# Two-term matmuls for five of fc2's sixteen groups, with the scales applied to the sum in PSUM, and every y_hi copy on ScalarE

## The reference

```
attn_in = tanh(x @ W1 + b1)                       # 512 -> 128
scores  = attn_in @ v
p       = softmax(where(mask, scores, -1e30))     # prefix, postfix or cloze mask by sequence
pooled  = (p @ x) / count(mask)
h       = layernorm(pooled) * gamma + beta
y       = silu(h @ dequant(fc1_q, fc1_scales) + fc1_bias)      # 512 -> 2048
z       = y @ dequant(fc2_q, fc2_scales) + fc2_bias            # 2048 -> 512
out     = x + pooled + 0.5 * z
# dequant: (q - 128) * scale, one scale for each group of 128 rows of the weight and each column
```

## Time and profile before

| | |
|---|---|
| median of 3 runs | 1396.38 us (1396.19 to 1396.42) |
| the profiled execution | 1397.07 us, its span 1395.4 us |
| PE busy | 1362.2 us (98% of the span), 6243 matmuls |
| DVE busy | 967.0 us (69%) |
| ACT busy | 895.6 us (64%) |
| POOL busy | 198.7 us (14%) |
| granted TensorE clock | 0.994 of full on average |

### The profile page before, as it was taken

One profiled execution on the slowest core, in us unless ns is written; L12 is line 12 of the kernel. 1 busy time (PEld: TensorE's weight loads), 2 busy tenths in 40 slices (PEclk: granted clock), 3 DMA queues, 4 the chain that ended last, 5 costly groups with the idle time before them and its releaser, 6 DMA issues.

```text
span 1395.4 us, 20229 instructions
## 1 busy us (share of the span) xinstructions
PE 1362.2 (98%) x6243; PEld 1075.6 (77%) x6243; DVE 967.0 (69%) x1923; ACT 895.6 (64%) x1415; POOL 198.7 (14%) x156
## 2 busy tenths in 40 slices
...
DMA packets 271437, 82.15 MB, mean 59 GB/s; under 512 B 247530, under 2 KB 248196, under 8 KB 270852
## 3 DMA queue, kind: packets, MB, share of 16 engines
...
...
## 4 chain that ended last, share of the span: by engine, by line
PE 66%; SPq 16%; DVE 10%; issue 5%; DMA 3%; ACT 1%; ACTq 0%; DVEq 0%
PE y_ps L1110 12%; PE z_ps L1137 11%; PE y_ps L1111 11%; PE z_ps L1139 11%; PE z_ps L1138 11%; SPq L394 10%; SPq L349 6%; DMA h_cols<-scratch 2%; DVE h_rows L862 2%; DVE hT_lo L874 1%; PE a_ps L1020 1%; PE a_ps L1069 1%; PE a_ps L1071 1%; PE a_ps L1070 1%; PE a_ps L1021 1%
## 5 line engine op out<-in xcount | busy, mean ns | idle before, releaser
L600 ACT ACTIVATE y_ps<-y_ps,ratio 128x512 f32<-128x512 f32 x768 | 474.7, 656 | 342.0 <-PE y_ps L1111 340.3
L1110 PE MATMUL y_ps<-hT_hi,w 128*128 128x512 f32 x1016 | 403.1, 397 | 15.6 <-DVE hT_lo L874 8.9
L1137 PE MATMUL z_ps<-w_hi,y_hi 128*128 128x512 f32 x1024 | 409.4, 400 | 0.0
L1139 PE MATMUL z_ps<-w_hi,y_lo 128*128 128x512 f32 x1024 | 400.2, 391 | 0.0
L1138 PE MATMUL z_ps<-w_lo,y_hi 128*128 128x512 f32 x1024 | 400.1, 391 | 0.0
L1111 PE MATMUL y_ps<-hT_lo,w 128*128 128x512 f32 x1016 | 396.9, 391 | 0.0
L904 DVE CAST y_hi<-y_f 128x512 fp32r<-128x512 f32 x248 | 120.5, 486 | 263.9 <-ACT y_f L594 161.9
L1110 PEld LDWEIGHTS y_ps<-hT_hi,w 128*128 128x128 f32 x1016 | 191.3, 188 | 76.7 <-issue 13.9
L594 ACT ACTIVATE y_f<-y_ps,vec_cols,mant 128x512 f32<-128x512 f32 x256 | 185.2, 775 | 94.3 <-PE y_ps L1111 92.3
L1137 PEld LDWEIGHTS z_ps<-w_hi,y_hi 128*128 128x128 f32 x1024 | 192.9, 188 | 58.7 <-issue 19.4
L1138 PEld LDWEIGHTS z_ps<-w_lo,y_hi 128*128 128x128 f32 x1024 | 192.8, 188 | 42.7 <-issue 3.6
...
## 6 DMA issues: line engine op xcount, KB each, us to landing
...
```

The costliest lines, as they stand in the source:

```text
L600: nc.scalar.activation(y_ps[k % 2][:], y_ps[k % 2][:], ACT.Copy, scale=ratio[:, c * NF + k:c * NF + k + 1]).then_inc(scaled, 1)
L1110: mm(o, w, hT_hi[:, c, :], start=(c == 0), stop=False, skip_group_check=True)
L1137: mm(z_ps[r][:], y_hi[k % 2][:, rows], w2_hi[:, k, :], start=(k == 0), stop=False)
L1139: last = mm(z_ps[r][:], y_lo[k % 2][:, rows], w2_hi[:, k, :], start=False, stop=(k == NF - 1))
```

## The change

Groups 1, 6, 7, 10 and 11 of fc2 (WHOLE) are done like fc1: their weight holds (q - 128) times a power of two, exact in fp32r, so the hi by lo matmul (L1138) is left out for them. After each of these groups VectorE multiplies the whole sum so far, in PSUM, by a ratio of mantissas (`rescale_z`, four multiplications of 128x512 a group). The weights of the groups between them are divided by the mantissa that is still to come, and the factor 0.5 moves into these units. VectorE, GpSimd and one DMA to device memory make the units in the prologue (`scale_masks`, units_dram), and the units and ratios are loaded from there. The first of two row blocks is multiplied one slot after its matmuls, the other in the slot behind that; fc2 of the next group waits for them (z_scaled).

All y_hi copies move to ScalarE: for one group behind the two SiLUs, for the other at the start of the second slot after. VectorE's `split_y` keeps the subtraction. GpSimd's bias waits for h_ready instead of hT_done, in sequence 0 for more of fc2. In sequence 0 the steps L2 and W2 of the five groups go.

```diff
+    WHOLE = (1, 6, 7, 10, 11)
+    EARLY = 3
+    SEGMENTS = ((0, 1, 1), (2, 6, 6), (8, 10, 10))
...
-        DVE_LATE = {0: [("L2", 1), ("D1", 4)], 1: [("D2", 2)], 3: [("L2", 2)], 4: [("D2", 4)], 5: [("D1", 6)], 6: [("L2", 4)],
+        DVE_LATE = {0: [("D1", 4)], 1: [("D2", 2)], 3: [("L2", 2)], 4: [("D2", 4)], 5: [("D1", 6)], 6: [("L2", 4)],
...
             load_w1(0)
+            sp.wait_ge(units2, 1)
+            sp.dma_start(units_dram.rearrange("k (p j) -> p k j", p=Q), u2_c).then_inc(units2_out, 16)
+            sp.wait_ge(units2_out, 16)
+            load_w2_units(0)
+            load_ratios(z_ratio[:], 0, EARLY)
...
                 if J == 0 and is_first(a):
-                    pool.wait_ge(fc2_done, 4)
+                    pool.wait_ge(fc2_done, 10)
                 elif J == 0:
-                    pool.wait_ge(hT_done, a * ND + ND)
+                    pool.wait_ge(h_ready, a * NJ + NJ)
...
+            pool.wait_ge(masks2, 1)
+            for k0, k1, k in SEGMENTS:
+                step(g.tensor_tensor(u2_c[:, k0:k1, :], s2_c[:, k0:k1, :], i2_c[:, k:k + 1, :].to_broadcast([Q, k1 - k0, NC]), ALU.mult))
...
-            def y_hi_part(k):
-                act.wait_ge(silu_done, k + 1)
-                if k >= 2:
-                    act.wait_ge(fc2_done, k - 1)
-                copy(y_hi[k % 2][:], y_f[k % 2][:]).then_inc(yhi_even, 1)
+            def y_hi_part(b, k):
+                act.wait_ge(silu_done, b * NF + k + 1)
+                if k >= 2 or not is_first(b):
+                    act.wait_ge(fc2_done, b * NF + (k - 1))
+                copy(y_hi[k % 2][:], y_f[k % 2][:]).then_inc(yhi_done, 1)
...
                     ahead, k, c = fc1_slot(i)
+                    if i % 4 == 0:
+                        y_hi_part(b, i // 2 + 1)
...
-                    if is_first(b) and c == ND - 1 and not ahead:
-                        y_hi_part(k)
+                        if c == ND - 1:
+                            y_hi_part(b + ahead, k)
...
+            def scale_masks():
+                dve.wait_ge(s2_in, 16)
+                bits, mants = s2_c.bitcast(I32), m2_c.bitcast(I32)
+                link(v.tensor_scalar(u2_c[:, 0:NF, :].bitcast(I32), bits, 23, 23, ALU.logical_shift_right, ALU.logical_shift_left))
+                link(v.tensor_scalar(mants, bits, 9, 9, ALU.logical_shift_left, ALU.logical_shift_right))
+                link(v.tensor_tensor(mants, mants, ones[0:Q, 0:1].bitcast(I32).rearrange("p (k j) -> p k j", j=1).to_broadcast([Q, NF, NC]), ALU.bitwise_or))
+                v.reciprocal(i2_c, m2_c).then_inc(masks2, 1)
...
             def split_y(b, k):
-                dve.wait_ge(silu_done, b * NF + (k + 1))
-                if k >= 2 or not is_first(b):
-                    dve.wait_ge(fc2_done, b * NF + (k - 1))
-                if is_first(b) and k % 2 == 0:
-                    dve.wait_ge(yhi_even, k // 2 + 1)
-                else:
-                    v.tensor_copy(y_hi[k % 2][:], y_f[k % 2][:]).then_inc(yhi_done, 1)
-                    dve.wait_ge(yhi_done, (k + 1) // 2 if is_first(b) else b * NF + (k + 1) - NH)
+                dve.wait_ge(yhi_done, b * NF + k + 1)
                 v.tensor_tensor(y_lo[k % 2][:], y_f[k % 2][:], f32(y_hi[k % 2][:]), ALU.subtract).then_inc(split_done, 1)
+
+            def rescale_z(b, k, r):
+                if r < NJ - 1:
+                    dve.wait_ge(z_part, z_part_count(b, k, r))
+                else:
+                    dve.wait_ge(fc2_done, b * NF + (k + 1))
+                if is_first(b) and r == 0:
+                    dve.wait_ge(ratio_in, 16 if WHOLE.index(k) < EARLY else 32)
+                v.tensor_tensor(z_ps[r][:], z_ps[r][:], z_ratios[WHOLE.index(k)], ALU.mult).then_inc(z_scaled, 1)
...
                 for i in range(SLOTS):
-                    if i % 4 == 0:
-                        split_y(b, i // 2 + 1)
                     if i % 4 == 3 and i < SLOTS - 1:
                         split_y(b, (i + 1) // 2)
+                    if (i - 1) // 2 in WHOLE:
+                        for r in (2 * ((i - 1) % 2), 2 * ((i - 1) % 2) + 1):
+                            rescale_z(b, (i - 1) // 2, r)
+                    if i % 4 == 0:
+                        split_y(b, i // 2 + 1)
...
                 if k == 0 and not is_first(b):
                     pe.wait_ge(final_done, (b - 1) * NJ + (r + 1))
+                if k - 1 in WHOLE:
+                    pe.wait_ge(z_scaled, z_count(b, k - 1, r))
                 rows = slice(r * P, (r + 1) * P)
-                mm(z_ps[r][:], y_hi[k % 2][:, rows], w2_hi[:, k, :], start=(k == 0), stop=False)
-                mm(z_ps[r][:], y_hi[k % 2][:, rows], w2_lo[:, k, :], start=False, stop=False)
-                last = mm(z_ps[r][:], y_lo[k % 2][:, rows], w2_hi[:, k, :], start=False, stop=(k == NF - 1))
+                mm(z_ps[r][:], y_hi[k % 2][:, rows], w2_hi[:, k, :], start=(k == 0), stop=False, skip_group_check=True)
+                if k not in WHOLE:
+                    mm(z_ps[r][:], y_hi[k % 2][:, rows], w2_lo[:, k, :], start=False, stop=False, skip_group_check=True)
+                last = mm(z_ps[r][:], y_lo[k % 2][:, rows], w2_hi[:, k, :], start=False, stop=(k == NF - 1 or k in WHOLE), skip_group_check=True)
```

More of the change, by code:

```diff
@@ L127, in small @@
             return columns4[:, k * NJ:(k + 1) * NJ]
+        z_ratio = sb("z_ratio", [P, EARLY, D])
+        z_ratios = [z_ratio[:, j, :] for j in range(EARLY)] + [e1[1][:, j, :] for j in range(len(WHOLE) - EARLY)]
+        units_dram = nc.dram_tensor("units_dram", [NF + len(WHOLE), D], F32, kind="Internal").ap()
+        NC = D // Q
+        s2_c, m2_c, i2_c = (h_rows[0:Q, 1 + n, 0:NF * NC].rearrange("p (k j) -> p k j", k=NF) for n in range(3))
+        u2_c = h_rows[0:Q, 0, 0:(NF + len(WHOLE)) * NC].rearrange("p (k j) -> p k j", j=NC)
         pen_c = small()
@@ L230, in build @@
         powers_out = sem("powers_out")
+        s2_in = sem("s2_in")
+        masks2 = sem("masks2")
+        units2 = sem("units2")
+        units2_out = sem("units2_out")
+        ratio_in = sem("ratio_in")
+        z_part = sem("z_part")
+        z_scaled = sem("z_scaled")
         fc1_done = sem("fc1_done")
@@ L386, in _ @@
                 load_w2(g)
+            for k0 in w1_unit:
+                if k0 // NG == 1:
+                    sp.wait_ge(w1_unit[k0], 1)
+            sp.wait_ge(ratio_in, 16)
+            load_ratios(e1[1][:, 0:len(WHOLE) - EARLY, :], EARLY, len(WHOLE))
             def move_h(a):
```

58 lines of the change are left out of this document (39 added, 19 removed).

## The result

The changed kernel takes 1426.93 us (median of 4 runs, 1424.87 to 1431.66) against 1396.29 for the kernel before: ratio 1.0226, 95% interval [1.0211, 1.0241]. It is 2.3% slower. The profiled execution took 1431.66, its span is 1429.9, 34.5 more than before. It is the slowest of the four: they took 1431.66, 1427.27, 1426.60 and 1424.87 at mean granted clocks of 0.975, 0.980, 0.983 and 0.984.

The account below looks back on a forecast made before the run. It took PE's matmuls and a fixed DMA chain from slot 16 to 27 as bounds side by side. 1395.4 - 1.4 (14 sequences) - 4.5 (last) + 5 (prologue, sequence 0) + 1.5 (waits) gave span 1396, forecast 1397.5 us, range 1374 to 1421.

Parts of the forecast that it names:

- Cost of a multiplication of z: On DVE, one multiplication of z in PSUM takes 0.60 us, like the final addition; bounds 0.55 and 1.66.
- Rival (d): A multiplication in PSUM costs 0.72 us instead of 0.60; 12 on the path, +1.4 a sequence, 1418; chance 0.14.
- Slots 2 to 8: Group 1's multiplications delay y_lo(4), for which slot 8 waits: 1.04 us longer a sequence instead of 0.91 shorter.
- Rival (a): DVE keeps up better, slot 8 not waiting for y_lo(4): 1370 to 1383, or 1360; chance 0.22.
- Slots 12 to 16: PE saves 8 matmuls, 1.81 us a sequence; full DVE delays the last split of x, stall 0.36.
- Slots 16 to 27: xs_used 0.6 us earlier, but h waits for normalisation; slot 27 starts 0.07 earlier, PE waits there about 2.9.
- the chain: Fixed stretch from the column DMAs after slot 16 through the h DMAs and transposes to slot 27; 24.3 us before.
- rival c: The pause before slot 27 lowers TensorE's clock: 1.3 us in each of 14 sequences, 18 in all, 1416; chance 0.15.
- Slots 27 to 2: The y_hi(15) copy adds 0.27 us at slot 29; moving GpSimd's bias takes 0.3 off; -0.03 a sequence.
- Prologue and sequence 0: Making the units and 14 multiplications on a full DVE cost +5 us together, believable from +2 to +9.
- last sequence: With no conditioning work beside it, the last sequence saves its whole 4.53 us of matmuls.
- The sum itself: Over the whole kernel: 1395.4 - 1.4 - 4.5 + 5 = 1394.5, plus 1.5 for forgotten waits; said 1397.5.

Follow-up runs that it names:

- e9: The changed kernel with group 1 back to three matmuls, so four groups with two (6, 7, 10, 11): 1435.12 us, ratio 1.0288.
- e5: The changed kernel with GpSimd's residual addition of block 2 made to wait for the last xs_lo: 1420.58 us, ratio 1.0173.
- e1: The changed kernel plus 8 idle matmuls on PE in slots 20 to 23 of sequences 1 to 14: 1419.03 us, ratio 1.0165.
- e4: The kernel before with every y_hi made by ScalarE, three matmuls for every group, bias not moved: 1406.22 us, ratio 1.0076.

## Why the prediction was wrong

It forecast 1397.5 with a range of 1374 to 1421; 1426.93 is above both. Two terms of its sum failed: the stall behind slots 12 to 16, which it put at 0.36 us and which is 1.29, and the clock behind slot 27, which it left out of the sum and which cost 17.8 us. By its own steps:

- **Cost of a multiplication of z**: right. 0.690 us each, 0.60 from start to start: two in 1.29 (DVE's rows above). Rival (d) is out.
- **Slots 2 to 8**: right. DVE began y_lo(2) at 681.58, 2.72 behind slot 2 (forecast 2.70), y_lo(4) at 694.56, 15.70 behind it (15.63). Slot 2 to 9 is 17.94 us against 16.83 before: +1.1, forecast +1.04. Rival (a) is out. e9 takes 0.6 of it away.
- **Slots 12 to 16**: the saving was right (1.81 forecast; slot 12 to 16 is 10.01 instead of 11.78, -1.77). **The stall of 0.36 behind it was wrong, it is 1.29** (18.0 / 14). I had the slow y_lo beside GpSimd in the earlier trace rows, and used it for the bias, but did not ask which other instruction the shift of DVE's queue would push under the residual additions. e5 takes 0.97 of it away; the 0.31 that are left (4.4 / 14) are what the 0.36 was worked out for.
- **Slots 16 to 27**: the structure was right, its start was not. Counted from slot 2 as in the prediction, xs_used comes 0.36 later than before instead of 0.6 earlier (the stall, 0.93). From there the chain is 0.66 longer than before, forecast 0.53. Between the first column DMA and the first h DMA lie 8.8 to 8.9 us in even sequences (8.78 in sequence 8), where h is late as forecast, and 9.3 to 9.6 in odd ones from 3 on (9.27 in sequence 7), where the column DMAs take 9.15 instead of 8.31; why they do is open. So slot 27 comes 1.02 later (14.3 over the five columns from slot 2) instead of 0.07 earlier. The pause was forecast at 2.9 and is 2.80 in sequence 7, 2.35 to 3.23 over the fourteen.
- **Clock behind slot 27** (rival c): I gave it 0.15 because the earlier trace rows shows a pause only together with transposes. **It came true, beside the forecast's own path and not instead of it**: in 10 of 14 sequences, 1.8 us each, 17.8 in all. That I had priced it at 18 is luck: 14 times 1.3. e1 shows it by removal. No transposes are needed for it.
- **Slots 27 to 2**: +0.2 at slot 29 (forecast +0.27) and -0.35 in slots 0 to 2 (-0.3), right; but e4, where the bias is not moved, has about half of the latter, so that it is not shown to be the bias alone. The rest, 2.6 in slot 31 and about 1 in slots 0 to 2, is PE's instruction queue, which no step named.
- **Prologue and sequence 0** +5.6 (forecast +5), **last sequence** -4.4 (-4.5): right.
- **The sum itself**: its terms at slot 27 (-0.56, +0.72, -0.2) give -0.04 and not -0.07, and 1397.7 less the 0.7 of the median is 1397.0 and not 1397.5; neither matters beside the 29 us missed.

In sum, over 14 sequences I forecast -1.4 and they gave +33.3. Of the 34.7 between them, 13.0 are the stall (0.93 x 14), 17.8 the clock, 3.6 PE's instructions and 2.3 the slower column and h DMAs; 2.0 go the other way in the slots behind 27. The steps that failed are the stall behind slots 12 to 16, where an xs_lo pushed under GpSimd's addition takes 1.66 us instead of 0.69, and the clock behind slot 27, rival (c), which I had treated as an alternative and which came on top. Without the clock's part the profiled execution would have taken 1413.9 (1431.7 - 17.8), still above the forecast's own range of 1390 to 1406.
